# A recommender tower on one core: 24 more row steps in chunks 3 and 4, top layers in seven visits, and GpSimd's additions one by one between the gathers

## What is computed

```python
e = jnp.stack([tbl_f[ids[:, f]] for f in range(40)], axis=1)   # 2048 x 40 x 64
i_idx, j_idx = np.triu_indices(40, k=1)                        # 780 pairs
viW = jnp.einsum('bpd,pde->bpe', e[:, i_idx, :], W)
z = jnp.einsum('bpe,bpe->bp', viW, e[:, j_idx, :])
h = jnp.concatenate([z, dense_ctx], axis=1)                    # 796 columns
h = jnp.maximum(h @ W_top1 + b_top1, 0.0)                      # 512
h = jnp.maximum(h @ W_top2 + b_top2, 0.0)                      # 256
y = h @ W_top3
```

## Time and profile before

| | |
|---|---|
| median of 3 runs | 1622.22 us (1618.03 to 1629.02) |
| profiled execution, its own time | 1626.08 us |
| its span | 1623.9 us |
| mean granted TensorE clock | 0.949 |
| PE busy | 1478.4 us, 91% |
| DVE busy | 973.7 us, 60% |
| ACT busy | 872.0 us, 54% |
| POOL busy | 735.6 us, 45% |
| chain that ended last | PE 87%, issue 8%, DVE 2% |

### The profile page before, as it was taken

One profiled execution on the slowest core, in us unless ns is written; L12 is line 12 of the kernel. 1 busy time (PEld: TensorE's weight loads), 2 busy tenths in 40 slices (PEclk: granted clock), 3 DMA queues, 4 the chain that ended last, 5 costly groups with the idle time before them and its releaser, 6 DMA issues.

```text
span 1623.9 us, 52519 instructions
## 1 busy us (share of the span) xinstructions
PE 1478.4 (91%) x21300; PEld 676.9 (42%) x21300; DVE 973.7 (60%) x841; ACT 872.0 (54%) x6611; POOL 735.6 (45%) x891
## 2 busy tenths in 40 slices
PE   5788988878888999989999999999999999999999
PEld 2245555534555433333334443334333453433333
DVE  2564555535555554666666565667666655679991
ACT  0633443445554573465766564354656634448992
POOL 5433433354444343436556554445655544452320
PEclk7787989979999999999999999999999999999999
DMA  4232322223232122212222221222222121221200
GB/s 120 63 114 60 82 67 69 74 61 81 70 81 58 46 56 61 69 40 62 56 49 56 48 55 46 68 66 55 62 53 53 49 54 44 63 81 55 61 10 13
DMA packets 60957, 98.79 MB, mean 61 GB/s; under 512 B 17062, under 2 KB 17078, under 8 KB 60715
## 3 DMA queue, kind: packets, MB, share of 16 engines
q1 hardware_dynamic: 35876, 65.08, 13.8%
q0 software_dynamic: 20224, 20.75, 6.8%
q10 hardware_dynamic: 4614, 9.61, 1.8%
HBM read 95.37 MB, written 0.01 MB: 59 GB/s over the span
## 4 chain that ended last, share of the span: by engine, by line
PE 87%; issue 8%; another core or an unknown queue 2%; DVE 2%; ACT 0%; DMA 0%; ACTq 0%; DVEq 0%
PE u L1176 36%; PE u L1162 22%; PE zacc L1190 17%; PE u L1232 5%; PE u L1105 3%; PE u L1249 2%; DVE prod L1060 1%; PE u L1121 1%; PE u L1220 1%; PE u L1208 0%; DVE row_prod L1029 0%; DMA h<-tbl 0%; ACT row_prod L920 0%; ACT emb L874 0%
## 5 line engine op out<-in xcount | busy, mean ns | idle before, releaser
L920 ACT ACTIVATE row_prod<-row_prod 128x64 f32<-128x64 f32 x3248 | 777.2, 241 | 218.5 <-DVE row_prod L1029 179.6
L1176 PE MATMUL u<-emb,weights 64*32 64x512 f32 (+1 forms) x9760 | 773.4, 530 | 58.7 <-issue 45.1
L1060 DVE TENSOR_TENSOR prod<-u,emb 128x1024 f32<-128x1024 f32 x496 | 593.4, 1218 | 383.4 <-remote 193.6
L807 POOL DMA_INDIRECT gathered<-tbl,index x512 | 483.8, 945 | 608.1 <-DVE prod L1060 248.8
L920 ACT ACTIVATION_READ_ACCUMULATOR row_prod<-row_prod 128x1 f32 x3248 | 609.7, 188 | 5.1 <-issue 4.8
L1162 PE MATMUL u<-row_weights,emb 64*32 64x512 f32 (+5 forms) x5632 | 492.1, 539 | 38.4 <-issue 26.9
L1176 PEld LDWEIGHTS u<-emb,weights 64*32 64x32 f32 x9760 | 292.2, 110 | 389.8 <-issue 285.0
L1190 PE MATMUL zacc<-prod,band 64*32 64x512 f32 (+1 forms) x4960 | 407.4, 521 | 21.9 <-issue 19.0
L1029 DVE TENSOR_TENSOR row_prod<-u,first_fields 128x1024 f32<-128x1024 f32 x203 | 247.0, 1217 | 156.2 <-PE u L1162 90.7
L1162 PEld LDWEIGHTS u<-row_weights,emb 64*32 64x32 f32 x5632 | 161.5, 109 | 242.6 <-issue 160.1
L1190 PEld LDWEIGHTS zacc<-prod,band 64*32 64x32 f32 x4960 | 164.4, 110 | 164.6 <-issue 149.0
(11 more groups left out here) (41 smaller groups left out, 221.8 us busy)
## 6 DMA issues: line engine op xcount, KB each, us to landing
weights<-w_pairs SPq DMA_DIRECT2D x155, 256.0 KB
row_weights<-w_rows SPq DMA_DIRECT2D x90, 256.0 KB
gathered<-tbl,index POOLq DMA_INDIRECT x512
w12s<-w_top ACTq DMA_DIRECT2D x8, 832.0 KB
w12s<-w_top ACTq DMA_DIRECT2D x4, 512.0 KB
first_fields<-tbl,index POOLq DMA_INDIRECT x120
h<-tbl SPq DMA_DIRECT2D x2, 224.0 KB
h<-tbl ACTq DMA_DIRECT2D x2, 224.0 KB
```

What stands on the lines that cost most here:

```text
L807: pool.indirect_dma_start(out=to, out_offset=None, in_=tables[2 * t + e], in_offset=bass.IndirectOffsetOnAxis(ap=index[:, col:col + 1].bit ...
L920: last = nc.scalar.activation(x, x, ACT.Copy, accum_out=row_sums[:, c % 2, s, q:q + 1])
L1060: nc.vector.tensor_tensor(result, products, x, ALU.mult).then_inc(prod_ready, 1)
L1176: last = nc.tensor.matmul(u[of, b, h, to], weights[half, x % WRING, unit, of], y, start=True, stop=True)
```

## The change

It touches the planning part above all; the program text of the engines follows from it.

**More rows.** `KIND` = (0, 0, 1, 1): chunks 3 and 4 have another set of steps, 100 column and 96 row steps. The 24 new row steps take the pairs of tiles 8 to 19 with tiles 4 and 5, which are kept too (`KEPT` = 6), in a new double buffer `more_fields`. Such a step (of the tiles `XS`) has 16 matmuls of 256 columns instead of 8 of 512. To make room in the memory, the ring of gathered tiles has 3 slots instead of 4.

**Reducers.** `VECTOR_RING` is 3 and `POOL_EVERY` is (4, 4, 4, 2). Rows by chunk for ScalarE, VectorE, GpSimd: before 53/19/0, 54/8/10, 48/8/16, 48/8/16; now 53/19/0, 43/21/8, 57/21/18, 38/21/37.

**Seven visits.** Each visit of the top layers now makes one block of 128 outputs. They stand at steps 217, 240, 255, 271, 287, 313, 332, then 430, 450, 470, 489, 513, 532, 552, then 630, 650, 670, 689, 708, 727, 746. In chunks 1 and 2 layer 1 has 256-column matmuls (two per block of rows), in chunks 3 and 4 seven matmuls of 512 columns. Weights come in pieces of 448 and 256 KB where they came in 832 and 512 KB. The dense inputs of chunks 3 and 4 are put into `z` by a DMA.

**GpSimd's queue.** The six additions of a reduction stand one by one, with a gather between two of them where one is due by `LEVEL_SPACE` = 3 steps after the product.

```diff
-VECTOR_RING = 2
+VECTOR_RING = 3
-POOL_EVERY = 4
+POOL_EVERY = (4, 4, 4, 2)
+LEVEL_SPACE = 3
-GRING = 4
+GRING = 3
+KEPT = 6
+MORE = range(2 * FT, 2 * KEPT)
+FIRST_X = 30
+XS = range(FIRST_X, FIRST_X + (T - 2 * FT) // 2)
+KIND = (0, 0, 1, 1)
-TOP_GROUPS = M1 // 2 + M2 // 2 + 1
+TOP_GROUPS = M1 + M2 + 1
...
-        new = [("col", k, t) for k in range(HUB + 1, t)]
+        new = [("col", k, t) for k in range(hub + 1, t) if kind == 0 or t < 2 * FT or k not in (KEPT, KEPT + 1)]
...
+for j, x in enumerate(XS):
+    a, b = 2 * FT + 2 * j, 2 * FT + 2 * j + 1
+    RUNS[x] = tuple(((2 * a + h, 0, len(MORE)), (2 * b + h, len(MORE), FF)) for h in (0, 1))
+    AGAINST[x] = [*MORE, *MORE]
...
+def make_row_steps(kind):
+
+    tiles = [1, 0]
+    for t in range(FT, T):
+        tiles.append(t)
+        if kind and t > 2 * FT and t % 2:
+            tiles.append(XS[(t - 2 * FT) // 2])
+    return [("row", t, s) for t in tiles for s in range(SUB)]
...
-TOPS = [(1, 0), (1, 2), (2, 0), (3, 0)]
+TOPS = [(1, m) for m in range(M1)] + [(2, m) for m in range(M2)] + [(3, 0)]
...
-    on_pool = set(others[POOL_EVERY - 1::POOL_EVERY])
+    on_pool = set()
+    for c, every in enumerate(POOL_EVERY):
+        others = [x for x in rows if x >= POOL_FROM and x // N == c and x not in on_vector]
+        on_pool.update(others[every - 1::every])
...
     for x in ON_POOL:
         place = max([i for i, o in enumerate(out) if o[0] <= x + 1], default=-1) + 1
-        out.insert(place, (x + 1, "reduce", x))
+        for i in range(len(LEVELS)):
+            out.insert(place, (x + 1, "reduce", x, i))
+            place += 1
+            if place < len(out) and out[place][0] <= x + LEVEL_SPACE:
+                place += 1
...
+                        if KIND[c]:
+                            last = nc.tensor.matmul(u[:, b, 0, :], w12s[:, x % 2, q, :], z_blocks(c, q)[:, 0, :],
+                                                    start=(q == 0), stop=(q == ZG - 1))
+                            continue
+                        for h in (0, 1):
+
+                            half = slice(h * DIM, (h + 1) * DIM) if q == ZG - 1 else slice(0, P)
+                            at = slice(h * CB // 2, (h + 1) * CB // 2)
+                            last = nc.tensor.matmul(u[:, b, h, 0:CB // 2], w12s[half, x % 2, q, :],
+                                                    z_blocks(c, q)[half, 0, at], start=(q == 0), stop=(q == ZG - 1))
```

More of the change, by code:

```diff
@@ L202, in make_first @@
     for q in range(PARTS):
-        twos = [("two", *COLUMN_STEPS[m:m + 2], q) for m in range(0, N_COLUMNS, 2)]
-        rows = [("row", x[1], q * SUB // PARTS + x[2] // PARTS) for x in ROW_STEPS if x[2] % PARTS == 0]
+        twos = [("two", *COLUMN_STEPS[0][m:m + 2], q) for m in range(0, N_COLUMNS[0], 2)]
+        rows = [("row", x[1], q * SUB // PARTS + x[2] // PARTS) for x in ROW_STEPS[0] if x[2] % PARTS == 0]
         mixed = []
@@ L834, in _ @@
                 else:
-                    reduce_row(o[1])
+                    reduce_row(o[1], o[2])
         @block.scalar
@@ L1216, in top_group @@
                 if layer == 1:
-                    def remainder(start):
-                        for m in (0, 1):
-                            half = slice(m * DIM, (m + 1) * DIM)
-                            last = nc.tensor.matmul(u[:, b, m, :], w12s[half, x % 2, 2 * FULL, :], z_blocks(c, FULL)[half, 0, :],
-                                                    start=start, stop=not start)
-                        return last
-                    if first:
-                        remainder(True)
@@ L1227, in top_group @@
-                    for m in (0, 1):
-                        for q in range(FULL):
-                            if first + m == 0:
-                                pe.wait_ge(z_copied, Z_COPY[(c, ROW_BLOCK, 0) if q >= ROW_BLOCK else
-                                                            (c, q // 2, len(parts(c)) - 1)])
-                            last = nc.tensor.matmul(u[:, b, m, :], w12s[:, x % 2, m * FULL + q, :], z_blocks(c, q)[:, 0, :],
-                                                    start=(first == 0 and q == 0), stop=(first > 0 and q == FULL - 1))
-                        if first and m == 0:
-                            last.then_inc(top_half, 1)
```

353 lines of the change are left out of this document (187 added, 166 removed).

## The result

The changed kernel is slower, not faster: 1639.28 us in the median of 15 runs (1633.34 to 1644.52) against 1626.95 of the kernel before (15 runs, 1615.68 to 1635.07), a ratio of 1.0086 with a 95% interval of 1.0067 to 1.0105. Forecast was 1.1% faster. The profiled executions have spans of 1623.9 and 1635.3 us, a difference of 11.4.

A forecast was written before the change was run, and what follows sets the result against it. Strings of gathers slowing TensorE, and VectorE after the last gather, were taken as bounds. 1619.1 without gather changes, +16, 0, -17 and -11 gave 1607; less 3.9, median 1604 us, 1.1% faster; range 1572 to 1642.

The forecast's parts named there:

- Without any change at the gathers: ... = 1619.1: Whole kernel: 1626.1 profiled, with row steps, smaller matmuls, moved visits and the end summed, gives 1619.1 us before gather terms.
- the -12, -5 and -11: Gathers: chunk 3 gains 12 us by additions separating them and 5 by visits covering strings; chunk 4's gather part gains 11.
- A row step has no sums: -10.3: Chunk 3: 24 more row steps, each saving 0.43 us of array time for sums, make it 10.3 us shorter.
- -4.4: Chunk 4's gather part: 10 more row steps without sums save 4.4 us of array time.
- ScalarE isn't the bound of chunk 3 either: Chunk 3: ScalarE, busy 207 of 373 us with 48 reductions, comes to at most 246 with 57.
- Chunk 3, -24 forecast: Chunk 3: row steps -10.3, smaller matmuls +3, spread gathers -12 and visits over strings -5 us.
- Chunk 4 with gathers, -26 forecast: Chunk 4's gather part: 150 us for 177, by fewer sums, fewer visits there and spread gathers.
- rival B: Chunk 4's gather part: GpSimd falls behind, VectorE waits for `row_prod_p`, TensorE for VectorE; median 1618, within 1%; chance 0.20.
- After the last gather, +14 forecast: Chunk 4's rest: twelve VectorE reductions of 1.21 us and a short wait at the visit add 14 us.
- The ring of 3, +16 forecast in chunk 1: Chunk 1: waits for ring slots make gathers 7 us late and longer strings cost 9; bounds 0 and +40.
- rival C: Ring strings of 7 and 8 find no cover and TensorE's clock drops: slower, median 1650; chance 0.18.
- Chunk 2, 0 forecast: Chunk 2: ring waits +9 us, strings falling on visits' matmuls that don't mind -10, taken as 0.

The follow-up runs named there:

- e6: The changed kernel with GpSimd's six additions in a row again, on the chip where gathers cost: 1683.34 us, 1.0359 of the kernel before.
- e5: The changed kernel itself, run again on the chip where gathers cost: 1638.42 us, 1.0098 of the kernel before.
- e12: The changed kernel without the 24 more row steps, ring still 3, where gathers are free: 1.014 of the kernel before.
- e10: The changed kernel with a ring of 4 and 6 instead of 7 column-weight slots, where gathers are free: 1.0224 of the kernel before.
- e13: The changed kernel with ring of 4, 6 column-weight slots and no more rows, where gathers cost: 1558.55 us, 0.9743 of the kernel before.
- e14: The kernel before with only its additions one by one between gathers, where gathers cost: 1582.43 us, 0.9897 of the kernel before.
- e2: The kernel before with only its additions one by one between gathers, where gathers are free: 0.9985 of the kernel before.
- e11: The kernel before with only its additions one by one between gathers, where gathers are free, run again: 0.9994 of the kernel before.

## Why the prediction was wrong, step by step

**The step that failed** is the line "Without any change at the gathers: ... = 1619.1", with the -12, -5 and -11 that were taken off it. Weigh each of TensorE's records by its columns and its tile, 0.0536 us for 512 columns at 64*32; this is an estimate of what the array needs, and the rest of a stretch is its loss:

| | array before | array changed | loss before | loss changed | loss with additions in a row (e6) |
|---|---|---|---|---|---|
| chunk 3 | 258.9 | 249.0 | 113.9 | 115.7 | 144.1 |
| chunk 4, gathers | 130.6 | 114.5 | 46.6 | 46.1 | 61.6 |

The array work fell as forecast, by 9.9 and 16.1 us (10.3 and 16.4 in the sum). The loss was to fall by 14 and 10, and stayed. That is 25 of the 30 us; the start and chunk 1 give 12 more, and chunk 2 takes 10 back. Spreading the gathers was not overrated: from e6 to e5 (113.4 and 45.8) it brings 31 and 16. What it had to make good was put at nothing: with the additions in a row, the new rows, reducers and ring raise the loss by 30 and 15. Where gathers are free the 24 new rows alone raise it by 20 and 17, from 10.7 to 30.6 and from 7.0 to 24.0 (e12 to e10). On the recorded chip e5 is above e13 by 20 and 17 too, but in chunk 2, where both have the same rows, also by 9, so the rows' share there may be that much less.

**What bounds the kernel now:** right for the chip it was read from, and the price law of strings held about: on the average over the changed kernel's strings without a visit beside them, in chunks 2 and 3, three gathers in a row lose 2.3 to 2.7 us, four 3.4 to 4.0, five 5.2 to 6.0. But I took it for the machine's. It is one chip's; on the others the same gathers are free.

**"A row step has no sums: -10.3", "-4.4", and "ScalarE isn't the bound of chunk 3 either":** the array time does fall. But a total of busy time below the span says nothing of the order within: ScalarE's copies of `emb` and of the turned rows stand behind its reductions, and TensorE waits for them. Where gathers are free chunk 3 gets 9.5 us longer by the rows and the term's sign turns (e10 against e12). On the recorded chip the changed kernel shows 0.7 us of such waits in chunk 3, so there it is not this that ate the gain; what in the new rows does it there stays open.

**Chunk 3, -24 forecast, -8.2 measured.** The count of single gathers was right (44 for 46), their price was not: in the changed kernel the window of a single gather loses 0.52 us on the average of 40, in the kernel before 0.36 (19 of them), in e13 0.20 (37) and in e14 0.25 (27). I had taken 0 to 0.3. With strings of seven that lost up to 8.7 us instead, the 12 us of the spreading were used up. That the difference comes from the new row steps is likely, since e13 differs by them, but e13 also differs by the ring; it is argued, not shown. Nor need it be the gather that got dearer: such a window holds every loss, and e10 has 20 us of loss by the rows where a gather costs nothing. The prediction's own sign for this chunk, 345 us, leaves out the 3 us for smaller matmuls; its terms give 349.

**Chunk 4 with gathers, -26 forecast, -16.6 measured:** rival B's mechanism. 160.6 us is the figure above which I had named it. In this part VectorE waits for GpSimd's reductions, which it never did before:

```profile
DVE row_prod_p L1078 <- POOL row_sums L870: 9.3, 4, 3.9
```

9.3 us are nearly all of the 10 that were missing, and TensorE in turn shows 7.3 us of waits for VectorE's `row_prod_p`. e13, without the new rows, has no such wait, and this part takes 152.4 us there.

**After the last gather, +14 forecast, +16.0 measured;** the end +1.7 and +1.3. Right, with the wait at the layer-1 visit (3.12 us) being the "short wait".

**The ring of 3, +16 forecast in chunk 1, +23 measured, and +5.5 at the start:** the mechanism, the place (step 58) and the sign were right, the size was not. Two things were left out of the working. Six kept tiles in a kernel whose ring waits only after kept and ring tiles are filled make the first string 28 gathers instead of 24; 4 x 1.25 = 5 us before the first multiply. (e13, with ring 4 as well, has 32 and starts 11 us later than e14. Where gathers are free all kernels start at 21 to 22 us, whatever the length of the first string, so this delay belongs to the chip where gathers cost; and it comes with the kept tiles, not with the ring of 3.) And TensorE, all but idle in strings of 18 and 20, is granted 0.58 to 0.65 of its clock; the prediction knew this of rival C alone and put nothing into its own sum. Chunk 1 had 50 us more at the lower level. What these cost apart from the string itself no run shows.

**Chunk 2, 0 forecast, -9.8 measured:** the cover by seven visits may have been the stronger of the two terms that I had set equal, but this is argued. With the additions in a row (e6) 389.0 us were left, so the additions brought 2 of the 10; and between e14 and e13, four visits and seven at a ring of 4, this chunk moves by 1 us alone.

**The mode switches** priced beside the rule of the Trainium skill ("TensorEngine Tiling (Array Packing)", section "Tiling Modes": changing the mode drains TensorE) were not tested by themselves. Where gathers are free, chunk 2, with seven visits instead of four, takes 274.1 against 275.5 us, but its visits follow transposes; the four that don't stand in the stretch after the last gather, where VectorE's queue accounts for the whole length.

Rival C, with 0.18, had the right sign, and by its own mark (a median above 1638) the result is just C's; but chunk 1 stayed under the 510 us named for C, and chunk 2 got shorter, not longer. B's mark in chunk 4 (above 160) was passed by 0.6 us. So each of the two holds in its place, and the loss that comes with the new rows was in neither.

## What to carry to other kernels

A gain in array time counts only after every engine's queue has been walked for what stands behind the new work; totals of busy time don't show it. A shorter ring costs where its waits let work pile up behind them, here in chunk 1 alone, the part with the smallest steps; before saving memory there, lay the planned order on measured step times and count the strings. When several edits come in one change, take them apart: here two of them together (ring and rows, 56 us) cost more than the others brought (40 us), and the kernel without them is 2.6% faster than before.

## What the runs showed of the hardware

One and the same program (e2, e11, e14) takes 1582 us on one chip and 1138 and 1140 on two others; the kernel before takes 1626 or 1598 on the first and 1139 to 1141 on four others. Stretches without gathers agree to 0.1 us in 126.6. GpSimd issues a gather in the same time on both, 948 and 946 ns, but on the one chip TensorE slows down behind it, by 3.4 to 4.0 us for four in a row, and the granted clock over chunk 1 is lower (0.92 against 0.97). Even on that chip the time of the unchanged kernel moved, 1626 and then 1598 us. What makes that chip different no run shows. For a comparison it means that a change tuned to hide such stalls can have another sign elsewhere: the additions between gathers are worth 1.0% here and nothing there, the changed kernel with ring 4 and all its rows loses 2.2 to 2.5% there. The changed kernel itself was not run on those chips.
